# A graph network of four layers: the third layer's normalizing and the fourth layer's row map, as two stages and as one pipeline

## What is computed

```
x = ln(x + L0(x))      # linear map, then sum over edges
x = ln(x + L1(x))      # sum over edges, two-layer MLP, ln, relu
x = ln(x + L2(x))      # weighted sum, then twice: linear, batch norm, relu
x = ln(x + L3(x))      # attention over edges
```

```
h2 = relu(batchnorm(z))                  # statistics over all 6250 nodes
x  = ln(x + h2)                          # over the 256 features of a node
h  = leaky_relu(x @ w_W + w_b, 0.2)      # L3, per node
e_ij = h[i] . a1 + h[j] . a2 + edge term + a_b
```

## Time and profile before

| | us |
|---|---|
| runs: median, lowest, highest | 6961.44, 6958.57, 6962.66 |
| profiled execution: span | 5494.9 |
| median less span | 1466.5 |

### The profile page before, as it was taken

How to read it: one execution, slowest core, us unless ns; L and a number is a source line. 1 busy time by engine, 2 the same in 40 slices (tenths; PEclk the granted TensorE clock), 3 DMA queues, 4 the chain that set the end, 5 groups by cost and what they waited for, 6 DMA issues and landing times.

```text
span 5494.9 us, 71163 instructions
## 1 busy us (share of the span) xinstructions
PE 3536.2 (64%) x14107; PEld 2622.1 (48%) x14107; DVE 3566.7 (65%) x11740; ACT 1431.3 (26%) x4459; POOL 3860.8 (70%) x4043
## 2 busy tenths in 40 slices
PE   2878694135555555566666656566666578888887
PEld 2655462024444444455555534444444445555554
DVE  8888887335555555566666645555554667788887
ACT  0211110000000000000000022222224456777776
POOL 2777777777777777777777667777773077777774
PEclk8999896567778777888888878877778789999999
DMA  3323231023333333333333333333331133343334
GB/s 86 82 70 78 64 89 37 2 71 112 111 111 112 111 113 104 107 113 111 113 111 112 100 98 105 105 105 105 105 105 49 51 106 109 111 113 111 112 112 75
DMA packets 257376, 521.07 MB, mean 95 GB/s; under 512 B 88217, under 2 KB 128621, under 8 KB 257139
## 3 DMA queue, kind: packets, MB, share of 16 engines
q0 software_dynamic: 179984, 423.92, 27.6%
q1 hardware_dynamic: 77155, 94.66, 5.9%
HBM read 483.72 MB, written 34.57 MB: 94 GB/s over the span
## 4 chain that ended last, share of the span: by engine, by line
PE 36%; POOL 17%; DMA 17%; issue 12%; DVE 12%; ACT 4%; DVEq 2%; SPq 0%; ACTq 0%; POOLq 0%
PE ps L1213 21%; POOL ZT L690 12%; DMA ZT<-table,meta_src 9%; POOL rec_src L635 5%; DMA ZT<-table,meta_dst 5%; PE ps L1223 3%; PE ps L1208 3%; DMA ACC<-in_edge_attr 2%; DVE ZT L1695 2%; PE ps L1172 2%; PE ps L1228 2%; DVE meta_src L1730 2%; DVE X L2117 1%; PE ps L1380 1%; DVE meta_src L1733 1%
## 5 line engine op out<-in xcount | busy, mean ns | idle before, releaser
L690 POOL DMA_INDIRECT ZT<-table,meta_dst x1616 | 1542.1, 954 | 684.7 <-issue 337.8
L690 POOL DMA_INDIRECT ZT<-table,meta_src x1568 | 1485.0, 947 | 513.8 <-issue 323.0
L1213 PE MATMUL ps<-ZT,xT 128*128 128x256 f32 x4704 | 1528.3, 496 | 467.7 <-DMA ZT<-table,meta_src 309.9
L1213 PEld LDWEIGHTS ps<-ZT,xT 128*128 128x128 f32 x4704 | 1215.2, 261 | 789.2 <-issue 179.7
L1812 DVE TENSOR_TENSOR ACC<-ps,ACC 128x256 f32 x2352 | 997.9, 424 | 813.4 <-PE ps L1213 553.8
L635 POOL DMA_INDIRECT rec_src<-ZT x800 | 796.4, 995 | 329.2 <-issue 239.1
L1208 PE MATMUL ps<-ZT,sel_x 128*128 128x256 f32 x294 | 162.6, 652 | 700.4 <-DMA ZT<-table,meta_src 495.9
L2117 DVE SCALAR_TENSOR_TENSOR X<-X,corr,ps 128x256 f32 x832 | 397.7, 478 | 134.5 <-PE ps L1223 47.2
L1172 PE MATMUL ps<-ewW,xT 128*128 128x256 f32 x1600 | 454.5, 386 | 0.0
L1223 PE MATMUL ps<-ZT,xT 128*128 128x256 f32 x1664 | 403.9, 393 | 50.7 <-ACT xT L965 21.5
L1208 PEld LDWEIGHTS ps<-ZT,sel_x 128*128 128x128 f32 x294 | 65.8, 279 | 751.4 <-DMA ZT<-table,meta_src 283.6
(11 more groups left out here) (423 smaller groups left out, 4530.9 us busy)
## 6 DMA issues: line engine op xcount, KB each, us to landing
ACC<-in_edge_attr SPq DMA_DIRECT2D x200, 240.0 KB
ZT<-table,meta_dst POOLq DMA_INDIRECT x1616
ZT<-table,meta_src POOLq DMA_INDIRECT x1568
rec_src<-ZT POOLq DMA_INDIRECT x800
table<-X SPq DMA_DIRECT2D x98, 128.0 KB
table<-ZT SPq DMA_DIRECT2D x49, 128.5 KB
table<-z SPq DMA_DIRECT2D x12, 512.0 KB
out<-X SPq DMA_DIRECT2D x48, 128.0 KB
```

Source lines behind the costliest of these rows:

```text
L690: pool.indirect_dma_start(rows[:, s % depth, 0:width], None, table[layer], bass.IndirectOffsetOnAxis(ap=ids[:, s, 0:1].bitcast(I32), axis= ...
L1213: nc.tensor.matmul(slot_sum(j), sel[:, k % 2, j, :], ring[:, (2 + k) % RG * G + j, 0:D], start=True, stop=True).then_inc(sem["summed"], 1)
```

## The change

Both stages become one loop over s = 0 to 14 (on DVE 15), and the row map runs BEHIND = 2 batches behind the normalizing. PE does in a step `turn_rows(s-2)`, `turn_back(s)`, `map_rows(s-2)`; ACT `copy_columns(s-2)`, `bn_relu_1(s+1)`, `root_3(s)`, `relu_rows(s-2)`, `normalize_3(s)`; DVE `back(s)`, `neighbour_terms(s-3)`, `one_over(s)`. `turn_rows` writes to banks 4 and 5, and `map_rows` to banks 6 and 7 for every batch, where it waits for the banks to be used by the batch before. z lies in ACC instead of ZT (`mapped`), so that ht, which lies in ZT, can be written while later batches are still normalized. DVE's product sums with the second vector go straight to the 257th word of ht (the copies of s2 fall away), and those with the first vector are taken out of the loop: they follow it, last 40 tiles first. POOL's first 40 gathers of layer four wait, each, for one of these products (`h_step`). The loops on ACT and DVE, which were hardware loops, are written out.

```diff
+BEHIND = 2
+        def mapped(b, m):
+            n = min(SB, T - b * SB) * P if isinstance(b, int) else SB * P
+            o = b * (SB * D) + m * n
+            return ACC[:, o:o + n] if isinstance(b, int) else ACC[:, bass.ds(o, n)]
@@ gather (POOL)
                     if s >= depth:
                         ...
+                    elif layer == 3:
+                        pool.wait_ge(sem["h_step"], s + 1)
@@ ACT (lin2b, gather_stats on DVE: ztf[...] -> mapped(b, m))
+            def copy_columns(b):
+                n = min(SB, T - b * SB) * P
+                act.wait_ge(sem["xT_psum"], b + (XB[3] + 1))
+                act.wait_ge(sem["y_psum"], b + (YB[3] - 1))
+                for k in range(KC):
+                    nc.scalar.copy(xT[:, b % 2, k, 0:n], ps[:, 4 + k, 0:n]).then_inc(sem["xT_sbuf"], 1)
+            def relu_rows(b):
+                ...
+                act.wait_ge(sem["y_psum"], b + (YB[3] + 1))
+                y = psf[:, 512 * 6:512 * 6 + nt * D].rearrange("p (t d) -> p t d", d=D)
+                nc.scalar.activation(ht[:, b * SB:b * SB + nt, 0:D], y, ACT.Relu, scale=1.0 - SLOPE).then_inc(sem["h_relu"], 1)
-            batches(act, bn_relu_and_norm)
-            ...
-            staggered(act, copy_xT(3, "y_psum", YB[3]), relu_rows)
+            bn_relu_1(0)
+            for s in range(NB + BEHIND):
+                if s >= BEHIND:
+                    copy_columns(s - BEHIND)
+                if s + 1 < NB:
+                    bn_relu_1(s + 1)
+                if s < NB:
+                    root_3(s)
+                if s >= BEHIND:
+                    relu_rows(s - BEHIND)
+                if s < NB:
+                    normalize_3(s)
@@ PE
-            each_batch(turn_back)
-
-            pe.wait_ge(sem["back_used"], NB)
-            ...
-                rows_out(b, nt, lambda k, j: xT[:, q, k, j * P:(j + 1) * P], 0, 4 + 2 * q, YB[3] - 1, bias16[:, 0, :])
+            def turn_rows(b):
+                pe.wait_ge(sem["rows_done"], b + (ROWS[2] + 1))
+                pe.wait_ge(sem["xT_sbuf"], b * KC + XS[3])
+                for k in range(KC):
+                    for j in range(min(SB, T - b * SB)):
+                        mm = nc.tensor.transpose(ps[:, 4 + k, j * P:(j + 1) * P], acc3[:, b * SB + j, k * P:(k + 1) * P], ident[:, :])
+                mm.then_inc(sem["xT_psum"], 1)
+            def map_rows(b):
+                pe.wait_ge(sem["xT_sbuf"], (b + 1) * KC + XS[3])
+                rows_out(b, min(SB, T - b * SB), lambda k, j: xT[:, b % 2, k, j * P:(j + 1) * P], 0, 6, YB[3], bias16[:, 0, :])
+            for s in range(NB + BEHIND):
+                if s >= BEHIND:
+                    turn_rows(s - BEHIND)
+                if s < NB:
+                    turn_back(s)
+                ...
+                if s >= BEHIND:
+                    map_rows(s - BEHIND)
@@ DVE
+            def neighbour_terms(b):
+                nt = min(SB, T - b * SB)
+                dve.wait_ge(sem["y_psum"], b + (YB[3] + 1))
+                dve.wait_ge(sem["h_relu"], b + 1)
+                h = ht[:, b * SB:b * SB + nt, 0:D]
+                y = psf[:, 512 * 6:512 * 6 + nt * D].rearrange("p (t d) -> p t d", d=D)
+                v.scalar_tensor_tensor(h, y, SLOPE, h, ALU.mult, ALU.add).then_inc(sem["y_used"], 1)
+                dve.wait_ge(sem["y_used"], b + (YB[3] + 1))
+                wait(dve, sem["ht_ready"], b)
+                for j in range(nt):
+                    t = b * SB + j
+                    ins = v.scalar_tensor_tensor(other_out[:, 0, j, :], ht[:, t, 0:D], 1.0, bc[:, 2, :], ALU.mult, ALU.mult,
+                                                 accum_out=ht[:, t, D:D + 1])
+                ins.then_inc(sem["ht_ready"], 1)
+            for s in range(NB + BEHIND + 1):
+                if s < NB:
+                    back(s)
+                if s >= BEHIND + 1:
+                    neighbour_terms(s - BEHIND - 1)
+                if s < NB:
+                    one_over(3, back_last, s, norms(3)[:, s % 2], min(SB, T - s * SB), s + (ROWS[2] - 1))
+            dve.wait_ge(sem["ht_ready"], NB)
+            for t in (*range(T - R3 , T), *range(T - R3 )):
+                v.scalar_tensor_tensor(X[:, t, :], ht[:, t, 0:D], 1.0, bc[:, 1, :], ALU.mult, ALU.mult,
+                                       accum_out=s1[:, t:t + 1]).then_inc(sem["h_step"], 1)
+            dve.wait_ge(sem["h_step"], T)
             v.tensor_scalar(s1[:, :], s1[:, :], col[:, AB:AB + 1], None, ALU.add).then_inc(sem["s1_ready"], 1)
```

More of the change, by code:

```diff
@@ L1337, in _, with turn_back @@
             each_batch(lin2b)
-            def turn_back(b, q, nt):
+            def turn_back(b):
                 pe.wait_ge(sem["bn_applied"], (NB + b + 1) * KC)
                 wait(pe, sem["back_used"], b - 1)
-                for j in range(nt):
+                for j in range(min(SB, T - b * SB)):
                     for k in range(KC):
                         c = (j % 2) * D + k * P
-                        src = ztf[:, k, nodes(b, nt * P)][:, j * P:(j + 1) * P]
-                        mm = nc.tensor.transpose(ps[:, 2 * q + j // 2, c:c + P], src, ident[:, :])
+                        mm = nc.tensor.transpose(ps[:, 2 * (b % 2) + j // 2, c:c + P], mapped(b, k)[:, j * P:(j + 1) * P], ident[:, :])
@@ L2003, in _, with back @@
             back_step, back_last = norm_steps("ln_step2", 2), norm_steps("ln_step3", 1)
-            def back(b, q, nt):
-                rows = x_rows(own_tiles(mybir.EngineType.DVE, 0, nodes_of(b, nt)))
-                wait(dve, sem["back_psum"], b + 1)
+            def back(b):
+                nt, q = min(SB, T - b * SB), b % 2
+                rows = x_rows(own_tiles(mybir.EngineType.DVE, 0, slice(b * SB, b * SB + nt)))
+                dve.wait_ge(sem["back_psum"], b + 1)
                 for j, x in enumerate(rows):
-                    ins = v.tensor_tensor(tile_of(acc3, b, j), ps[:, 2 * q + j // 2, (j % 2) * D:(j % 2 + 1) * D], x, ALU.add)
+                    ins = v.tensor_tensor(acc3[:, b * SB + j, :], ps[:, 2 * q + j // 2, (j % 2) * D:(j % 2 + 1) * D], x, ALU.add)
@@ L2010, in back @@
                 ins.then_inc(sem["back_used"], 1)
[L2011 to L2025, removed]
+                dve.wait_ge(sem["back_used"], b + 1)
@@ L2026, in node_rows @@
+                row_stats(3, back_step, b, norms(3)[:, q], [acc3[:, b * SB + j, :] for j in range(nt)])
+            def neighbour_terms(b):
+                nt = min(SB, T - b * SB)
+                dve.wait_ge(sem["y_psum"], b + (YB[3] + 1))
+                dve.wait_ge(sem["h_relu"], b + 1)
+                h = ht[:, b * SB:b * SB + nt, 0:D]
+                y = psf[:, 512 * 6:512 * 6 + nt * D].rearrange("p (t d) -> p t d", d=D)
                 v.scalar_tensor_tensor(h, y, SLOPE, h, ALU.mult, ALU.add).then_inc(sem["y_used"], 1)
-                wait(dve, sem["y_used"], b + (YB[3] + 1))
+                dve.wait_ge(sem["y_used"], b + (YB[3] + 1))
+                wait(dve, sem["ht_ready"], b)
@@ L2036, in node_rows @@
-                h_step(b, ins)
-                v.tensor_copy(tiles(ht, b, nt)[:, :, D], s2[:, nodes_of(b, nt)]).then_inc(sem["ht_ready"], 1)
-            batches(dve, node_rows)
-            dve.wait_ge(sem["h_step"], NB)
+                    ins = v.scalar_tensor_tensor(other_out[:, 0, j, :], ht[:, t, 0:D], 1.0, bc[:, 2, :], ALU.mult, ALU.mult,
+                                                 accum_out=ht[:, t, D:D + 1])
+                ins.then_inc(sem["ht_ready"], 1)
+            dve.wait_ge(sem["weights_in"], WEIGHTS[3])
```

42 lines of the change are left out of this document (19 added, 23 removed).

## The result

The changed kernel takes 6963.94 us (median of 20 runs, 6951.21 to 6989.38) where the kernel before, run beside it, takes 6952.35 us (20 runs, 6940.23 to 6976.27): ratio 1.0022, 95% interval 1.0012 to 1.0032, that is +11.6 us between the medians and +8 to +22 us by the interval. The forecast was 6979 us, slower by 17.9. Slower is right; how much of the size is right has to be read from the stretch itself, since the whole profile moved for another reason.

A forecast was written before the change was run, and what follows sets the result against it. Attention was taken as paced by POOL's 832 gathers, starting once table[3]'s stores land, and the merged stages as bound by a chain around the engines. 17.1 + 0.8 = +17.9 us on a 6961.4 us median gave 6979 us, range 6951 to 6998.

The forecast's parts named there:

- Filling, turns, draining: Merged loop: 18.0 us until map 0 ends, nine turns of 13.8 us (124.2), then 20.3 us; 162.5 against 145.4.
- its two edges: Merged loop: back(s) ahead of the scaled sum in DVE's queue, and the single pair of map banks.
- The gap: PE before each map_rows: idle 5.1 us every step, until DVE's scaled sum releases the banks.
- The clock: PE in the loop: slow start at 1.2 GHz after each gap, 2.9 us a step, making 13.8 from 10.9.
- Behind the stores: Start of layer four's attention: 16.9 us of first-vector products delay DVE, mostly hidden; first round 0.8 us late.
- the ring: Slots for POOL's gathers: they cover 12 us of lateness, so POOL does not stop; 5 us if cover failed.
- Gathers beside products: POOL's first 14 gathers beside DVE's two-input products: 0 to 4.5 us, taken as 0.
- The sum: Whole change: 17.1 us until the stores are complete plus 0.8 us behind them, +17.9 us.
- The time around the span: Outside the profiled span: 1466.5 us of the 6961.4 us median, taken as unchanged by the change.
- with the clock up: Rival, merged loop: PE's clock stays up, -10 us, 6951 us, no change; chance 0.12.
- The rival with the loop open: Merged loop not closed: about 7.5 us a step, stretch 103.5 us, -42 us, 6920 us; chance 0.09.
- The rival of the late attention: Layer four's attention: 5 us of ring and 4.5 us of port come on top, +27 us, 6988; chance 0.09.

The follow-up runs named there:

- the short execution: The changed kernel, otherwise unaltered, run and profiled again beside the kernel before: 5521.98 us against 5508.42, ratio 1.0029.
- the products inside: Changed kernel with the 49 first-vector products back inside the loop: 5522.78 us, ratio to the kernel before 1.0027.
- the scaled sum first: Changed kernel with DVE doing neighbour_terms(s-3) ahead of back(s), still one pair of map banks: 5476.96 us, ratio to the kernel before 0.9963.
- two pairs of banks: Changed kernel with two pairs of map banks by turns and one pair for turned-back tiles: 5473.56 us, ratio to the kernel before 0.9961.
- the best kernel: Two pairs of map banks, and ACT normalizes batch s-1 behind the copy of batch s-2: 5445.07 us against 5496.72 before, ratio 0.9906.

## Why the prediction was right, step by step

- **Filling, turns, draining.** The prediction had 18.0 + 124.2 + 20.3 = 162.5 us. In the short execution of the changed kernel map 0 ends 18.2 us after the first add, map 9 ends 122.7 us later, and the last product 19.8 us after that: 160.8 us. The loop was named with its two edges, and cutting either one (122.7, 122.3 us) shows that both are needed.
- **The gap.** 5.1 us was worked out; 5.14 was found, released by the scaled sum's line.
- **The clock.** 2.9 us a step was taken between 0 and 5.5; the kernel whose gap is filled with work puts it at 2.7. The row with the most similar gap was a good guide, and the nine turns were oversized by 1.5 us in all.
- **Behind the stores.** Taken as 0.8 us for a late first round. The first round is 1.8 us later (39.5 against 37.7 us with the products inside), and the ring hides it: the gathers take 1050.7 us beside 1048 to 1051 in the five profiles in which DVE is ready early. The term should have been nothing; it is mis-sized, without a consequence.
- **Gathers beside products.** Taken as 0, between 0 and 4.5 us for 14 gathers. Only nine stand beside products, since these begin 4.9 us ahead of POOL and end 12.1 us behind its start: the first takes 1.24 us (1.01 without products), the others 1.03 to 1.08 instead of 0.95. With the gathers behind them the fifteenth start comes 1.45 us later (19.57 less 18.12), a third of the upper end that was taken from 4392.40. The page "SBUF — State Buffer" of the Trainium skill says in its section "Who interferes with whom" that a DVE instruction with two SBUF inputs contends with a GpSimd instruction that reads SBUF; for these products the trace agrees in the direction, with some 0.12 us a gather. The row at 4140.42 was read rightly and still did not carry over. In the profile of before 29 gathers stand mostly beside operations of that kind (L1892, two SBUF inputs), with a median of 0.95 us. So two SBUF inputs alone do not settle it, and what sets the products apart was not tried.
- **The sum.** 15.4 us of stretch (160.8 less 145.4) and 1.5 us of gathers make 16.9 us, where 17.9 were forecast. The medians of the timed runs say +11.6 and +13.6, with intervals of +8 to +22 and +9 to +22 us, which hold 16.9 without narrowing it.
- **The time around the span.** This assumption was wrong. The prediction took 1466.5 us as lying around the span in every execution; it is 1.8 us. The timed executions were long inside the span: 1074 us of it ahead of the stretch, and 366 us in the gathers of layer four, where POOL is held by PE's sums and no longer by its own issue. The 6979 us of the forecast rest on this wrong constant. The difference of 17.9 us survived because most of it lies in a stretch with no gather in it, which is as long in either kind (159.6 and 160.8 us). That is luck for the forecast of the timed runs, which were all of the long kind: the reasoning on POOL's issue was made for the other. The argument that lateness is hidden by the ring is shown for the short kind only. In the long kind the first attention matmul stands 57.6 us behind POOL's start, and what the late products add there was not tried; its ratio (1.0022) gives no sign of more.

The rivals: with the clock up a step is 10.93 us, as worked out, but it needed work in the gap. The rival with the loop open (a stretch of 103.5 us) is what the change could have been; the orders on DVE and on ACT kept it from that, one after the other. The rival of the late attention was to be decided by a wait of POOL over 0.3 us or gathers over 1 us in its first 17 us. In the short execution the second sign did come (1.03 to 1.43 us), and in the long one both, yet its +27 us did not: the sign was too weak, since one gather of 1.27 us stood in the rows of before already, and the short execution paid 1.5 us for its gathers and nothing for the ring.

## What to carry to other kernels

Two stages that are merged do not overlap by being in one loop: write down, for one step, who waits for whom through the in-order queues and the buffers, and look for a ring that closes once a step. Here two chains of 4.9 and 6.1 us became one of 10.9, and each wait that was cut uncovered another queue in which something not yet needed (`back`, then normalizing) stood ahead of what was. In such a loop, give each engine the work of the oldest batch first, and the work that waits for a partner's fresh result last or one step later. And where the timed median and the profiled span lie apart, suspect a longer execution before a constant around it.

## What was not expected of the hardware

- The same program takes some 5500 us on one occasion and some 6950 us on another, with spans to match. In the long kind ACT waits 608.9 us in the attention ahead of its copy (L982), 95 times, up to 11.6 us, for something the profile calls only remote (in the short kind that view has no such wait there), while single instructions keep their length (a gather 0.95 us). What it is stays open.
- PE's lower level does not need a gap as long as 5 us. In both kernels with a gap of 2.28 us in every full step (the scaled sum first, and two pairs of banks) three maps in four take 5.75 us and the fourth 4.07 us, behind the same gap and with the same work. In the kernel with two pairs of banks the granted clock was 1.00 over one map and 0.58 in the first 2 us of the next:

```profile
4298.20:4302.30 4.10, 4.06 (x22) 3.33 (x23) 3.70 (x14) 1.62 (x3) 0.00 (x0) 1.00 0.01 2
4306.40:4308.40 2.00, 2.00 (x7) 1.52 (x8) 1.82 (x9) 1.52 (x3) 0.00 (x0) 0.58 0.17 58
```

  In the best kernel, whose gaps ahead of full maps are 0.35 to 1.82 us, the clock was 1.00 from 4250 to 4330 us. What makes the difference between the maps no run here separates.
- Filling PE's gap with useless matmuls made the stretch 22.6 us shorter, more than the 19 us of work that they added.
